# Adding the residual in the last store: normalised rows go out by DMAs that add, and two experts run alone in place of four

## What is computed

```python
x = x + _layernorm(_L0_attn_ref(_layernorm(x), ...))      # RWKV recurrence, four 512x512 products
x = x + _layernorm(_L0_ffn_ref(_layernorm(x), ...))       # shared MLP + routed experts
# _L0_ffn_ref: scores = sigmoid(x @ gate_w.T); top 4 of 8 groups, top 6 of 64 experts
#   shared = relu(x @ su.T)**2 @ sd.T
#   routed = per expert (at most 128 tokens): relu(xd @ w1.T)**2 @ w2.T, times the gate,
#            added to the rows of its tokens
#   return shared + routed
```

## Time and profile before

| | |
|---|---|
| median of 3 runs | 1407.62 us (1406.45 to 1408.04) |
| the profiled execution | 1404.05 us, its span 1402.3 us |
| TensorE busy | 1180.5 us (84%) |
| VectorE, ScalarE, GpSimd busy | 794.6, 589.5, 284.0 us |
| q1, q0 | 155.93 MB (33.0% of 16 engines), 39.85 MB (13.8%) |
| experts' stage | from 875.8 us (first scatter issued) to 1337.5 us |
| end | from 1337.5 us to 1402.3 us |

### The profile page before, as it was taken

How to read it: one execution, slowest core, us unless ns; L and a number is a source line. 1 busy time by engine, 2 the same in 40 slices (tenths; PEclk the granted TensorE clock), 3 DMA queues, 4 the chain that set the end, 5 groups by cost and what they waited for, 6 DMA issues and landing times. The chain is left out here.

```text
span 1402.3 us, 15536 instructions
## 1 busy us (share of the span) xinstructions
PE 1180.5 (84%) x5024; PEld 773.5 (55%) x5024; DVE 794.6 (57%) x2013; ACT 589.5 (42%) x993; POOL 284.0 (20%) x278
## 2 busy tenths in 40 slices
PE   5998998989898976598989888999999999999400
PEld 3443443434343434377878776777777677777300
DVE  4689797988797989676767681122212221221036
ACT  3464565665565666432232322333333333333124
POOL 2000010201010102100000001332333333343157
PEclk9998999999999987799999998999999999999755
DMA  8201030202020232342121114987996997788997
GB/s 313 97 0 60 0 120 26 95 30 90 30 90 1 90 124 86 139 169 66 63 94 35 64 35 161 234 223 217 258 241 175 275 237 202 226 241 231 285 226 261
DMA packets 80654, 196.74 MB, mean 140 GB/s; under 512 B 10048, under 2 KB 10176, under 8 KB 79552
## 3 DMA queue, kind: packets, MB, share of 16 engines
q1 hardware_dynamic: 64128, 155.93, 33.0%
q0 software_dynamic: 16448, 39.85, 13.8%
HBM read 143.83 MB, written 51.94 MB: 140 GB/s over the span
## 5 line engine op out<-in xcount | busy, mean ns | idle before, releaser
L474 PE MATMUL bank<-mix_ring,weights 128*128 128x512 f32 x768 | 349.8, 613 | 24.7 <-ACT bank L789 15.8
L474 PEld LDWEIGHTS bank<-mix_ring,weights 128*128 128x128 f32 x768 | 149.4, 197 | 214.3 <-issue 208.2
L1560 DVE TENSOR_TENSOR run_max<-run_max 128x256 f32<-128x256 f32 x64 | 27.2, 425 | 218.2 <-ACT run_max L950 218.2
L1534 DVE TENSOR_TENSOR k_sb<-k_sb 128x512 f32<-128x512 f32 x64 | 48.1, 752 | 179.9 <-ACT k_sb L917 179.9
L1115 POOL DMA_INDIRECT ysh<-k_sb,mixf x64 | 101.6, 1588 | 197.3 <-DMA ysh<-k_sb,mixf 105.7
L481 PE MATMUL bank<-weights,rw 128*128 128x512 f32 x256 | 120.3, 626 | 21.9 <-ACT sr L753 12.4
L590 PE MATMUL bank<-h_high,ffn_w 128*128 128x512 f32 x256 | 113.8, 444 | 10.8 <-ACT k_sb L917 10.8
L1094 POOL DMA_INDIRECT xres<-h,mixf x48 | 47.9, 997 | 347.5 <-DVE mixf L1544 334.7
L917 ACT ACTIVATE k_sb<-bank 128x512 f32<-128x512 f32 x64 | 38.2, 597 | 181.3 <-PE bank L592 181.3
L607 PE MATMUL bank<-ffn_w,s_split 128*128 128x512 f32 x256 | 112.1, 438 | 0.0
L592 PE MATMUL bank<-h_high,ffn_w 128*128 128x512 f32 x256 | 101.2, 395 | 0.0
(11 more groups left out here) (210 smaller groups left out, 2057.6 us busy)
## 6 DMA issues: line engine op xcount, KB each, us to landing
wkv<-in_w SPq DMA_DIRECT2D x96, 512.0 KB, 4.4
state<-in_w SPq DMA_DIRECT2D x32, 512.0 KB, 4.4
xin<-h SPq DMA_DIRECT2D x15, 1024.0 KB, 5.6
xin<-in_x SPq DMA_DIRECT2D x8, 1024.0 KB, 5.3
xres<-in_x SPq DMA_DIRECT2D x8, 1024.0 KB, 5.3
x<-xres SPq DMA_DIRECT2D x8, 1024.0 KB, 6.6
weights<-x SPq DMA_DIRECT2D x8, 1024.0 KB, 10.9
h<-hb SPq DMA_DIRECT2D x7, 1024.0 KB, 4.3
```

The source lines that it names most:

```text
L474: mm = pe.matmul(bank[:, d, :], W(j)[:, ck, d * P:(d + 1) * P], mix_slot(4 * j + ck), start=(ck == 0), stop=(ck == CK - 1))
```

## The change

There is no scratch array x1 any more: `store_tail` writes x1 straight to `out`. At the end nothing loads x1, and neither GpSimd nor VectorE adds it. When ScalarE has normalised tile k, GpSimd issues a DMA that adds the tile's rows to what lies in `out` (`o_store`), which is x1. SyncE issues no store at the end; it waits for both sets of stores. `ALONE` goes from 4 to 2, so 62 experts are spread over the same 30 steps.

```diff
-ALONE = 4
+ALONE = 2
...
-                sp.dma_start(tile_of(x1_by_tile, tau), xres[:, :, :]).then_inc(S["x1_stored"], 16)
+                sp.dma_start(tile_of(out_by_tile, tau), xres[:, :, :]).then_inc(S["x1_stored"], 16)
...
-                k = e - (E - ALONE)
-                if k >= 0:
-                    sp.wait_ge(S["down_done"], SJ * NT)
-                    sp.wait_ge(S["e_down"], e)
-                    sp.wait_ge(S["x1_stored"], 16 * NT)
-                    for n in range(2 * k, 2 * k + 2):
-                        sp.dma_start(o_x[n], x1_by_tile[n]).then_inc(S[f"x1_loaded{n}"], 16)
...
-            for k in range(NT):
-                sp.wait_ge(S["o_ready"], ST // 2 * (k + 1))
-                sp.wait_ge(S["o_added"], ST // 2 * (k + 1))
-                sp.dma_start(out_by_tile[k], o_y[k]).then_inc(S["out_stored"], 16)
+            sp.wait_ge(S["x1_stored"], 16 * NT)
             sp.wait_ge(S["out_stored"], 16 * NT)
...
-            def o_add(k):
-
-                pool.wait_ge(S[f"x1_loaded{k}"], 16)
-                for s in range(ST // 2):
-                    pool.wait_ge(S["o_normed"], ST * k + s + 1)
-                    pool.tensor_tensor(o_y[k][:, s, :], o_y[k][:, s, :], o_x[k][:, s, :], ALU.add).then_inc(S["o_ready"], 1)
+            def o_store(k):
+
+                pool.wait_ge(S["o_normed"], ST * (k + 1))
+                pool.dma_start(out_by_tile[k], o_y[k], accum_op=ALU.add).then_inc(S["out_stored"], 16)
 
             for k in range(NT):
                 o_scale(k)
                 if k >= 1:
-                    o_add(k - 1)
-            o_add(NT - 1)
+                    o_store(k - 1)
+            o_store(NT - 1)
...
-            def o_add(k):
-
-                dve.wait_ge(S[f"x1_loaded{k}"], 16)
-                for s in range(ST // 2, ST):
-                    dve.wait_ge(S["o_normed"], ST * k + s + 1)
-                    dve.tensor_tensor(o_y[k][:, s, :], o_y[k][:, s, :], o_x[k][:, s, :], ALU.add).then_inc(S["o_added"], 1)
-
             for k in range(NT):
                 o_moments(k)
-                if k >= 1:
-                    o_add(k - 1)
-            o_add(NT - 1)
```

More of the change, by code:

```diff
@@ L121, in sandwich @@
         gather_index scatter_index xd_turned xdT_ready e_up e_relu e_square e_down e_gated added
-        out_stored ln4_stats ln4_moments ln4_rstd o_joined o_normed o_ready o_added""".split()
+        out_stored ln4_stats ln4_moments ln4_rstd o_normed""".split()
         names += [f"{n}{q}" for n, b in (("w1_loaded", WB), ("w2_loaded", WB), ("xd_loaded", EB)) for q in range(b)]
-        names += [f"{n}{k}" for n in ("ysh_loaded", "x1_loaded") for k in range(NT)]
+        names += [f"ysh_loaded{k}" for k in range(NT)]
         S = {n: sem(n) for n in names}
@@ L215, in sandwich @@
         o_y = [rw[:, :, :], xres[:, :, :], hT, wkv[:, 0:ST * C].rearrange("p (s c) -> p s c", s=ST)] + [m[:, :, :] for m in youts[ROUTED:]]
-        o_x = [weights[:, k, :].rearrange("p (s c) -> p s c", s=ST) for k in range(NT)]
         x_by_tile = t["x"].rearrange("(t s p) c -> t p s c", s=ST, p=P)
-        x1_by_tile = t["x1"].rearrange("(t s p) c -> t p s c", s=ST, p=P)
         h_by_tile = t["h"][0:N, 0:C].rearrange("(t s p) c -> t p s c", s=ST, p=P)
@@ L1671 @@
     aps = {n: nc.dram_tensor(f"in_{n}", a.shape, _mybir.dt.from_np(a.dtype), kind="ExternalInput").ap() for n, a in arrays.items()}
-    scratch = {"x1": (N, C), "h": (N + P, C + E), "ysh": (N + P, C)}
+    scratch = {"h": (N + P, C + E), "ysh": (N + P, C)}
     aps.update({n: nc.dram_tensor(n, shape, F32, kind="Internal").ap() for n, shape in scratch.items()})
```

## The result

| | before | changed |
|---|---|---|
| median | 1407.21 us (14 runs, 1399.44 to 1413.63) | 1413.47 us (14 runs, 1408.24 to 1416.15) |
| profiled execution, span | 1404.05, 1402.3 us | 1410.57, 1408.8 us |
| GpSimd's queue | 39.85 MB | 48.24 MB |
| SyncE's queue | 155.93 MB | 139.16 MB |

The ratio is 1.0048, with a 95% interval of 1.0034 to 1.0063. A second set of 12 runs beside other kernels gave 1.0029 (1.0013 to 1.0044). The forecast was 1413.2 us. The total is right, but not each term: one was 5.8 us too low, another 4.3 us too high. In the two profiled executions the end stage, from GpSimd's first load of it to the end of the span, starts 5.8 us earlier (1331.67 for 1337.49) and takes 12.3 us longer (77.1 for 64.8).

A forecast was written before the change was run, and what follows sets the result against it. Bound: the scatter chain's lag, then DMA first and compute later. End start 1325.9 + loads 36.6 + stores 8 x 5.6 + landing 0.6 = 1407.9 us, 1413.2 on the median; range 1400 to 1436.

The forecast's parts named there:

- The store that adds: End stage, GpSimd's queue: eight 1 MB adding stores after the last load, at 5.6 us per MB (bounds 2.8 and 8.3).
- the forecast's own bracket: Adding stores at the end cost 5.2 to 6.6 us per MB, giving 1410 to 1421 us; chance 0.48.
- the draw: Adding stores at 4.6 to 5.2 us per MB, or an end starting at 1320: gains cancel cost, 1407.6 us; chance 0.10.
- The start of the end: When the chain of scatters has landed and the end stage begins: 1325.9 us, from 1320 to 1332.
- The chain's step: One scatter in the tail, without x1 loads beside it: 5.3 us, five of them from 1300.63 on.
- added for ALONE: Scatter chain, two experts alone instead of four: gains a 5.3 us step, loses 4.1, so 1.2 us earlier.
- a sign that steps with three experts cost something: Experts' stage: these steps cost nothing unless ScalarE waits for an older expert's addition; up to one 6.4 us step.
- The loads: End stage: the last load, xin, lands 36.6 us after the start, at 1362.5 us.
- The last landing: End of the span: 0.6 us added after the eight adding stores.
- The nearly free addition: Rival for the end's stores: adding costs 2.8 us per MB like plain stores, 1390.8 us on the median; chance 0.22.
- the wait in every packet: Rival for the end's stores: from one queue alone they cost 8.3 us per MB, 1434.8 us on the median; chance 0.20.
- The cover named for the issues on GpSimd: End stage: the last tile's store is queued near 1373, the queue reaches it at 1401.7, so 29 us hide compute.

The follow-up runs named there:

- the kernel with plain stores: The changed kernel with its eight last stores overwriting instead of adding, still issued by GpSimd: 1391.34 us, ratio 0.9895.
- the one with plain loads and four alone: The changed kernel with ALONE = 4 and the four adding ysh loads made plain, VectorE adding them: 1397.59 us, ratio 0.9934; again 1400.5 us, 0.9937.

## Why the prediction was right, term by term

*The store that adds* was the step that decides, and its mechanism holds: the DMA engines move an adding byte at half the rate of a plain one, and the end is theirs. The term was mis-sized by a tenth, 5.06 us per MB in place of 5.6, 4.3 us over the eight. It was read from small scatters; the adding load, 5.4, was nearer. The lone scatter's 8.3 does not carry over to long transfers: from one queue alone they run at a share of 1.13. That it was the lone scatter's start was argued and stays so.

The size matters for how the prediction is read. 5.06 lies outside the forecast's own bracket (5.2 to 6.6) and inside that of the draw (4.6 to 5.2). With every other term as forecast it gives 1407.9 - 4.3 = 1403.6, which is 1.3 us above before and within what the prediction itself called too small to tell.

*The start of the end* was put at 1325.9 and was 1331.7, and this makes up the rest. Three parts of it can be counted. The chain's step was taken as 5.3 near the one lone step of 4.95, and it is 5.7: 5 x 0.4 = 2 us. The first of the five scatters, at 1300.63 before, was expected no later and came at 1303.23: 2.6 us. And 1.2 us were added for ALONE, of which the runs show nothing: with four alone and no loads the end starts no later than with two, within the spread. The prediction also took TensorE's end to stay near 1314; it was 1320.2. It named a sign that steps with three experts cost something, ScalarE waiting for the addition of an expert four back. That wait is there, 8.0 us in six places, but the kernel before had 6.7 us in five, so it does not account for the difference. Why the chain came 2.6 us later stays open. Counted from the first gating the kernel before had the shortest TensorE part of all profiled ones, 439.5 us, and it is the one from which the sum was made.

The bound for this term was misread too: from 1198.57 to 1300.63 there are 15 steps, not 16, of 6.8 us on average, not 6.38. With that step the five would have ended at 1334.6. The whole gain in the chain is 5.8 us in these two executions, where 11.6 were written down; of these, 10.4 were for the loads, which with four alone are worth 4.6 to 5.4.

*The loads* ended 35.0 us after the start in place of 36.6, as an adding load alone takes 5.1 us per MB (sr lands at 1333.30 + 28.3 = 1361.6 and xin at 1366.7). *The last landing* to the end of the span took 1.6 us, not 0.6.

The sum of the errors is + 5.8 - 1.6 - 4.3 + 1.0 = + 0.9, and 1407.9 + 0.9 is the span measured. That the median came within 0.3 us is luck: a start too early and a store too dear cancelled. That it came out clearly slower, and not as a draw, rests on the late start as much as on the dear addition. With the start as late as it was, even 5.06 us per MB leaves the changed kernel behind: the break-even is (1402.3 - 1366.7 - 1.6) / 8 = 4.25, not 4.9. The nearly free addition is refuted by the kernel with plain stores, the wait in every packet by the pitch of the landings. The cover named for the issues on GpSimd (29 us) was there: 26 us lie between the last issue and the end.

## What to carry to other kernels

A DMA that adds moves a byte at half the rate of one that copies, on a target in device memory (207 GB/s for 419) as in on-chip memory (5.1 to 5.4 us per MB for 2.6 to 2.8). By these prices an adding store (5.06 us per MB) costs the DMA engines about what the load and the plain store that it replaces cost together (2.5 to 2.8 each). It saves next to none of their time; it moves the load's share to where the store stands, and that loses where the load cost little (here 4.6 to 5.4 us for all eight). Where the DMA engines set the end, give additions to a VectorE that has time, and put the cheap transfers last. A chain of small dependent transfers is lengthened by large ones issued beside it, even when the engines look half idle: its steps of 5.7 us left the DMA engines at a share of 0.40 (1305 to 1330 us of the changed kernel), and one 1 MB load in a step still made it up to 7.0 us long.

```profile
q0 software_dynamic: 649, 1.20, 40.0%
```

## What the runs showed that was not expected

GpSimd's plain 1 MB stores ran from one queue at 419 GB/s, in packets of 3.9 KB (1088 for 4.19 MB), and adding ones at 207 in packets of 2 KB. The share of the DMA engines rises to 1.13 with adding transfers and 1.02 to 1.06 with plain ones, so a share over 1 is no measure of bytes. The start of the experts' stage moved by 8 us between executions (869.3 to 877.5), and these two are executions of one and the same kernel, the one with plain loads and four alone. That is more than the whole effect of the change.
